# A graph layer on one core: three panels share the first groups of rows, and the late pieces of normalisation follow a new plan

## The chip, the cores and the metric

The kernel runs on one core of one Trainium2 chip. The metric is the device time of one execution in microseconds, as the median of several runs; lower is better.

## The reference

x is 8192 x 128, adj is 8192 x 8192 of zeros and ones (about one in 1024 is a one).

```
h    = relu(layernorm(x))                       # over the 128 features
deg  = max(adj.sum(axis=1), 1);  dis = deg ** -0.5
diff = (dis[:,None] * adj * dis[None,:]) @ h - h
sim  = h @ h.T / (|h_i| |h_j|)                  # cosines of all pairs of rows
attn = softmax(beta * sim * adj, axis=1)
out  = x + diff + sigmoid(alpha) * (attn @ h - h)
```

## The kernel before

The 8192 output rows are cut into 8 panels of 1024 (PANELS), the 8192 source rows into 4 groups (ch) of 16 tiles of 128. A **unit** is one panel with one tile of sources: a block of 128 x 1024 pairs. There are 512 units, numbered n = 0 to 511. ORDER lists (panel, group) for each chunk of 16 units, RUNS lists the stretches of chunks that keep one panel's accumulator in PSUM (panel, first chunk, end). Panels 0 and 1 share the first source group, so that the work can start before the other groups are normalised; where a panel's accumulator has been left, ScalarE has copied it to SBUF (`copy_acc`), and VectorE adds the later part (`add_acc`).

Each unit goes through the engines like this, always one instruction per step, with two or four buffers:

- TensorE, `cosines(n)` (L822): six 512-column matmuls of the unit vectors u, kept as fp16 head and tail (uT_hi, uT_lo), into one of two halves of cos_ps.
- VectorE, `masked(n)` (L693): the cosines times the adjacency bytes, to xm.
- ScalarE: two exponentials of it, the fp16 head (L418) and fp32 (L422).
- GpSimd, `rest(n)` (L325): the tail of the exponential by subtraction.
- TensorE, `sums(n)` (L867, L869, L871), called three units later (LAG): 24 matmuls that add e times h into the panel's accumulator.

Between these, VectorE transposes each block of adjacency words (`turn`, L630, every fourth unit) and sums the adjacency rows for the degrees (`sum_rows`, L637: 8 pieces a chunk, 256 in all; `sum_bytes` after every four chunks). GpSimd issues the row loads (L304, 8 a chunk, from `first_unit(k)` on) and makes the tails of h (L316, at the units of `tails`). SP stores the transposed adjacency and, by `keep_h`, h.

The first two groups of h are made ahead of the loop. The **late pieces** are the same steps for the others, put between units: `stats_of_x` (L508) and `mean_var` (L513) of x, a rough root on ScalarE (`var_root`) refined by `late_scale`, relu on ScalarE (L367, one tile a unit), `head_of_h` on ScalarE (L377), `stats_of_h` (L531) and `mean_var_of_h` (L536), `late_square_sums`, `ssq_root`, `late_norms`, `late_unit_rows` (L599), and at the units of AHEAD the transposition on TensorE (L798) of 1024 unit rows into the free half of cos_ps, copied from there by VectorE as head and tail (`copy_uT`, L606 and L607). The small steps pass through late_ps, a piece of PSUM. The order is written out by hand, by unit number: each engine runs its own loop over n. Ahead of the loop, TensorE runs WARM matmuls on the identity (L878, two passes each).

When all units are done, the roots of the degrees are made and a second phase (L901), 512 matmuls a panel, gives the diffusion. It is not touched by the change.

## Time and profile before

| | |
|---|---|
| median of 3 runs | 1890.43 us (1889.03 to 1893.34) |
| the profiled execution | 1890.3 us, span 1888.2 us |
| mean granted TensorE clock | 0.997 |
| busy: TensorE, VectorE, ScalarE, GpSimd | 97%, 66%, 68%, 67% |
| first cosine, last masked product | 38.88 us, 1426.26 us |
| second phase starts | 1436.65 us |

The span runs from the first to the last instruction. Matmuls overlap in their pipeline, so the busy time of one line of TensorE is more than its share, and the distance of starts is the better measure. The clock is given as a part of full speed (2.4 GHz).

### The profile page before, as it was taken

What the parts mean: (1) busy time and instruction counts of PE and PEld (TensorE: products, weight loads), DVE (VectorE), ACT (ScalarE), POOL (GpSimd) and SP (SyncE); (2) the same over time, 40 slices, a digit from 0 to 9 for tenths busy, and PEclk for the clock granted to TensorE, in tenths of its full rate; (3) what the DMA queues carried; (4) which work ended last, traced back from release to release, by engine and by line L of the source; (5) the groups of instructions that cost most, each with busy time, mean ns of one, the idle gap of its engine ahead of it and who ended that gap; (6) DMA issues with size and microseconds to landing.
All of it is one profiled execution on the core that took longest, in us unless ns stands there. A gap on an engine that the chain in (4) does not pass through costs nothing.

```text
span 1888.2 us, 44938 instructions
## 1 busy us (share of the span) xinstructions
PE 1835.1 (97%) x19614; PEld 1453.3 (77%) x19614; DVE 1253.8 (66%) x1591; ACT 1274.9 (68%) x1202; POOL 1272.0 (67%) x793
## 2 busy tenths in 40 slices
PE   4899999999999999999999999999998999999999
PEld 3667667777777777777777777777777888888888
DVE  7988997888787778778777877787876210111111
ACT  4879988888889889988998898898886000000000
POOL 4878899999999999999999999999882000000000
PEclk9999999999999999999999999999999999999999
DMA  9976877778896778888876778888436744555520
GB/s 153 171 90 91 135 91 96 96 95 105 102 127 91 102 93 100 107 101 104 105 101 90 102 95 100 107 101 108 99 108 251 242 171 162 198 177 175 205 101 12
DMA packets 190409, 229.39 MB, mean 121 GB/s; under 512 B 7940, under 2 KB 163588, under 8 KB 186116
## 3 DMA queue, kind: packets, MB, share of 16 engines
q0 software_dynamic: 135168, 67.13, 45.6%
q1 hardware_dynamic: 29380, 145.77, 21.3%
q10 hardware_dynamic: 25664, 13.63, 2.6%
q8 instruction: 153, 2.51, 0.5%
q14 instruction: 44, 0.36, 0.1%
HBM read 352.32 MB, written 75.50 MB: 227 GB/s over the span
## 4 chain that ended last, share of the span: by engine, by line
PE 87%; DVE 4%; ACT 3%; POOL 3%; issue 2%; DMA 0%; SPq 0%; DVEq 0%; POOLq 0%
PE cos_ps L822 31%; PE cos_ps L901 12%; PE top_ps L901 12%; PE top_ps L867 11%; PE top_ps L871 11%; PE top_ps L869 10%; POOL ustage L325 2%; ACT xe L422 1%; ACT ustage L418 1%; DVE xe L693 1%; DVE top_ps L637 1%; ACT asb L367 1%; PE cos_ps L878 1%; DVE ptmp L508 0%; POOL arena L304 0%
## 5 line engine op out<-in xcount | busy, mean ns | idle before, releaser
L325 POOL TENSOR_TENSOR ustage<-xe,ustage 128x1024 f16<-128x1024 f32 x512 | 1097.2, 2146 | 145.1 <-ACT xe L422 138.4
L693 DVE TENSOR_TENSOR xe<-cos_ps,arena 128x1024 f32<-128x1024 f32 x512 | 626.5, 1224 | 248.2 <-PE cos_ps L822 159.7
L418 ACT ACTIVATE ustage<-xe,ebias,ab 128x1024 f16<-128x1024 f32 x512 | 635.5, 1241 | 150.5 <-DVE xe L693 149.0
L867 PE MATMUL top_ps<-h,ustage 128*128 128x129 f16 x4096 | 720.6, 220 | 10.7 <-POOL ustage L325 7.3
L871 PE MATMUL top_ps<-h,ustage 128*128 128x129 f16 x4096 | 720.0, 220 | 0.0
L869 PE MATMUL top_ps<-hlo,ustage 128*128 128x128 f16 x4096 | 719.6, 219 | 0.0
L422 ACT ACTIVATE xe<-xe,ebias,ab 128x1024 f32<-128x1024 f32 x512 | 628.7, 1228 | 1.3 <-POOL ustage L325 1.2
L867 PEld LDWEIGHTS top_ps<-h,ustage 128*128 128x128 f16 x4096 | 401.4, 98 | 73.2 <-POOL ustage L325 17.0
L869 PEld LDWEIGHTS top_ps<-hlo,ustage 128*128 128x128 f16 x4096 | 401.3, 98 | 56.6 <-issue 0.6
L871 PEld LDWEIGHTS top_ps<-h,ustage 128*128 128x128 f16 x4096 | 401.3, 98 | 0.0
L822 PE MATMUL cos_ps<-uT_hi 128*128 128x512 f16 x1024 | 306.2, 381 | 13.1 <-DVE uT_lo L607 7.4
L637 DVE TENSOR_REDUCE top_ps<-arena 128x8 f32<-128x1024 uint16 x256 | 311.7, 1217 | 0.0
L822 PE MATMUL cos_ps<-uT_hi,uT_lo 128*128 128x512 f16 x1024 | 306.0, 380 | 0.0
L822 PE MATMUL cos_ps<-uT_lo,uT_hi 128*128 128x512 f16 x1024 | 305.9, 380 | 0.0
L822 PEld LDWEIGHTS cos_ps<-uT_hi,uT_lo 128*128 128x128 f16 x1024 | 116.5, 114 | 105.7 <-issue 1.6
L822 PEld LDWEIGHTS cos_ps<-uT_lo,uT_hi 128*128 128x128 f16 x1024 | 116.2, 113 | 106.0 <-issue 1.6
L304 POOL DMA_DIRECT2D arena<-adj_in_dram x256 | 171.6, 671 | 7.5 <-DMA asb<-x_in 7.5
L630 DVE STREAM_TRANSPOSE arena<-arena 128x1024 uint32<-128x1024 uint32 x128 | 158.0, 1234 | 0.0
L773 DVE SCALAR_TENSOR_TENSOR ptmp<-top_ps,dis,ptmp 128x128 f32<-128x128 f32 x64 | 19.5, 347 | 189.4 <-PE top_ps L901 188.8
L773 DVE SCALAR_TENSOR_TENSOR ptmp<-cos_ps,dis,ptmp 128x128 f32<-128x128 f32 x64 | 19.5, 347 | 157.8 <-PE cos_ps L901 157.2
L901 PE MATMUL cos_ps<-uT_hi,arena 128*128 128x256 f16 x896 | 98.5, 273 | 2.8 <-DVE uT_hi L754 2.8
L822 PEld LDWEIGHTS cos_ps<-uT_hi 128*128 128x128 f16 x1024 | 87.1, 113 | 16.7 <-DVE uT_lo L607 8.1
(113 smaller groups left out, 1043.7 us busy)
## 6 DMA issues: line engine op xcount, KB each, us to landing
arena<-adj_in_dram POOLq DMA_DIRECT2D x256, 256.0 KB, 8.1
at_scratch<-arena SPq DMA_DIRECT2D x128, 512.0 KB, 4.5
arena<-at_scratch SPq DMA_DIRECT2D x26, 2048.0 KB, 8.8
xe<-at_scratch SPq DMA_DIRECT2D x6, 2048.0 KB, 8.7
h_scratch<-asb SPq DMA_DIRECT2D x16, 256.0 KB, 8.7
arena<-h_scratch SPq DMA_DIRECT2D x16, 256.0 KB, 6.4
ustage<-h_scratch ACTq DMA_DIRECT2D x8, 512.0 KB, 4.1
ptmp<-x_in ACTq DMA_DIRECT2D x8, 512.0 KB, 5.3
```

The source lines that it names most:

```text
L304: pool.dma_start(rows8[k % RS][C * q:C * (q + 1), of, :], adj_v[panel][:, of, 2048 * ch + 512 * q:2048 * ch + 512 * (q + 1)]).then_inc(row ...
L325: nc.gpsimd.tensor_tensor(elo[:, n % ES, :], ef[:, n % XS, :], ehi[:, n % ES, :], ALU.subtract).then_inc(elo_done, 1)
L418: nc.scalar.activation(ehi[:, n % ES, :], xm[:, n % XS, :], ACT.Exp, bias=ebias[:, 0:1], scale=ab[:, 1:2]).then_inc(ehi_done, 1)
L422: nc.scalar.activation(ef[:, n % XS, :], xm[:, n % XS, :], ACT.Exp, bias=ebias[:, 0:1], scale=ab[:, 1:2]).then_inc(ef_done, 1)
L630: nc.vector.transpose(at_words[:, w, :].rearrange("p (a r) -> p a r", r=32), rows_words[k % RS][:, :, 32 * w:32 * (w + 1)]).then_inc(at_re ...
L637: nc.vector.tensor_reduce(out=pairs_ps[:, of], in_=rows_pairs[k % RS][:, 8 * part:8 * (part + 1), :], axis=AX.X, op=ALU.add).then_inc(rows ...
L693: nc.vector.tensor_tensor(xm[:, n % XS, :], cos_ps[:, slot_of(n), :], at8[:, m % W, :, n % B], ALU.mult).then_inc(x_done, 1)
L822: last = nc.tensor.matmul(cos_ps[:, slot_of(n), q * HALF:(q + 1) * HALF].rearrange("p (w z) -> p w z", w=W), own(mine, s), columns(src, pa ...
L867: nc.tensor.matmul(top_ps[:, bank, col:col + P + 1], head, h1[:, s, 0:P + 1], start=(first and t % 3 == 0), stop=final, skip_group_check=True)
L869: nc.tensor.matmul(top_ps[:, bank, col:col + P], head, hlo[:, s, :], start=False, stop=final, skip_group_check=True)
L871: last = nc.tensor.matmul(top_ps[:, bank, col:col + P + 1], tail, h1[:, s, 0:P + 1], start=False, stop=final, skip_group_check=True)
L901: return nc.tensor.matmul(acc2[panel % 2][:, t, :], slot8[k % SL][:, j // B, t * P:(t + 1) * P, j % B], y[s // 32][:, s % 32, :], start=(s ...
```

## The change

- **Order.** Panel 2 joins panels 0 and 1 in the first two source groups. The third group is first used at unit 96 (before 64), the fourth at 112 (before 80). There are three runs that VectorE adds (ADDED) and three early ones that ScalarE copies. AHEAD moves from units 18, 22, 56, 60, 73, 77 to 22, 30, 66, 78, 98, 106.
- **Plan.** The row sums start at unit 8 (SUM_UNITS) and take a third place in four between units 142 and 181. Row loads, `tails`, `keep_h` and every late piece get units of their own from tables. The variance of the third and fourth group is made in two halves (`late_var`, `late_scale`, `late_shift`), and copied to PSUM first. Relu runs in two units of three.
- **Head copies.** For the six late transpositions ScalarE copies the head (`copy_head`), ahead of its exponentials of that unit; VectorE waits for it and makes the tail.
- **Square sums.** `square_sums` works on the means and second moments that bn_stats gives for the halves of a tile; the sixteen bn_aggr fall away, early and late. The statistics of h go to PSUM (hstats is a view of late_ps, which is bank 3 of top_ps).
- **Warm-up.** WARM 24 in place of 40.

The diff, with unchanged lines and the declarations of buffers and semaphores left out; the rest of what is left out are the columns in which `sum_bytes` puts the first three batches, and `panel < 3` in `cosines`:

```diff
--- before.py
+++ after.py
@@ -38,7 +38,7 @@
-    WARM = 40
+    WARM = 24
@@ -47,12 +47,17 @@
-    AHEAD = {18: 2, 22: 3, 56: 4, 60: 5, 73: 6, 77: 7}
-    ORDER = [(0, 0), (1, 0), (1, 1), (0, 1), (0, 2), (0, 3), (1, 2), (1, 3)] + [(p, ch) for p in range(2, PANELS) for ch in range(CH)]
-    RUNS = [(0, 0, 1), (1, 1, 3), (0, 3, 6), (1, 6, 8)] + [(p, CH * p, CH * (p + 1)) for p in range(2, PANELS)]
+    AHEAD = {22: 2, 30: 3, 66: 4, 78: 5, 98: 6, 106: 7}
+    ORDER = [(0, 0), (1, 0), (1, 1), (2, 1), (2, 0), (0, 1), (0, 2), (0, 3), (1, 2), (1, 3), (2, 2), (2, 3)]
+    ORDER += [(p, ch) for p in range(3, PANELS) for ch in range(CH)]
+    RUNS = [(0, 0, 1), (1, 1, 3), (2, 3, 5), (0, 5, 8), (1, 8, 10), (2, 10, 12)] + [(p, CH * p, CH * (p + 1)) for p in range(3, PANELS)]
+    ADDED = (3, 4, 5)
...
+    SUM_UNITS = [n for n in range(8, UNITS) if n % B in (0, 3) and n != 72 or n % B == 2 and 142 <= n < 182][:8 * CHUNKS]
@@ -256,8 +262,8 @@
-                if m in (13, 16):
-                    keep_h(2 if m == 13 else 3)
+                if m in (14, 21):
+                    keep_h(2 if m == 14 else 3)
@@ -326,10 +332,10 @@
-                return 16 * (k - RS) + (18 if k < 13 else 13)
-            tails = {7: 4, 9: 5, 11: 6, 13: 7, 48: 8, 50: 9, 52: 10, 54: 11, 64: 12, 66: 13, 68: 14, 70: 15}
+                return max(16 * (k - RS) + 13, SUM_UNITS[8 * (k - RS) + 7] + 1)
+            tails = {7: 4, 9: 5, 11: 6, 13: 7, 44: 8, 47: 9, 54: 10, 57: 11, 70: 12, 73: 13, 80: 14, 83: 15}
@@ -356,13 +362,13 @@
-            def var_root(g, groups=1):
-                of = slice(16 * g, 16 * (g + groups))
+            def var_root(g):
+                of = slice(16 * g, 16 * (g + 1))
...
-                act.wait_ge(ln_ready, min(g, 2) + 1)
+                act.wait_ge(ln_ready, g + 1)
@@ -394,9 +400,9 @@
-                if run in (0, 4):
-                    groups = 1 if run == 0 else CH
+                if run in (0, 2, 6):
+                    groups = {0: 1, 2: 2, 6: CH}[run]
@@ -407,11 +413,17 @@
+            def copy_head(hb, slot):
+                act.wait_ge(uT_done, hb + 1)
+                nc.scalar.activation(uT_hi[:, PW * hb:PW * (hb + 1)], cos_ps[:, slot, :], ACT.Copy).then_inc(uT_hi_copied, 1)
...
-                if n >= 16 and n - LAG + 1 == 16 * RUNS[run][2] and run not in (2, 3):
+                if n >= 16 and n - LAG + 1 == 16 * RUNS[run][2] and run not in ADDED:
...
+                if n in AHEAD:
+                    copy_head(AHEAD[n], (slot_of(n) + 1) % 2)
@@ -422,16 +434,17 @@
-                if n in (3, 5, 45, 47, 61, 63):
-                    head_of_h({3: 2, 5: 3, 45: 4, 47: 5, 61: 6, 63: 7}[n])
-                elif n in (11, 49, 66):
-                    ssq_root({11: 1, 49: 2, 66: 3}[n])
-                elif n == 24:
-                    var_root(2, 2)
-                if 29 <= n < 45:
-                    relu(2, n - 29, n - 28)
-                elif 45 <= n < 61:
-                    relu(3, n - 45, n - 44)
+                if n in (3, 5, 38, 51, 64, 76):
+                    head_of_h({3: 2, 5: 3, 38: 4, 51: 5, 64: 6, 76: 7}[n])
+                elif n in (7, 55, 87):
+                    ssq_root({7: 1, 55: 2, 87: 3}[n])
+                elif n in (17, 39):
+                    var_root({17: 2, 39: 3}[n])
+                if 25 <= n < 49 and n % 3 != 0:
+                    relu(2, (n - 25) // 3 * 2 + (n - 25) % 3, (n - 25) // 3 * 2 + (n - 25) % 3 + 1)
+                elif 52 <= n < 76 and n % 3 != 0:
+                    relu(3, (n - 52) // 3 * 2 + (n - 52) % 3, (n - 52) // 3 * 2 + (n - 52) % 3 + 1)
@@ -531,18 +544,17 @@
-            def mean_var_of_h(g):
-                for s in range(16):
-                    ins = nc.vector.bn_aggr(out=hv[:, 16 * g + s, :], in_=hstats[:, s, :])
-                return ins
-            def early_square_sums(g):
+            def square_sums(g):
...
-                link(mean_var_of_h(g))
-                link(nc.vector.tensor_tensor(ssq[:, of], hv[:, of, 0], hv[:, of, 0], ALU.mult))
-                link(nc.vector.tensor_tensor(ssq[:, of], ssq[:, of], hv[:, of, 1], ALU.add))
-                nc.vector.tensor_scalar(ssq[:, of], ssq[:, of], float(P), COS_EPS * COS_EPS, ALU.mult, ALU.max).then_inc(hvar_ready, 1)
+                halves = hstats.rearrange("p s (k m) -> p s k m", m=3)
+                link(nc.vector.tensor_copy(hmeans, halves[:, :, :, 1]))
+                link(nc.vector.tensor_tensor(hmeans, halves[:, :, :, 1], hmeans, ALU.mult))
+                link(nc.vector.scalar_tensor_tensor(out=hmeans, in0=hmeans, scalar=P / 2.0, in1=halves[:, :, :, 2],
+                                                    op0=ALU.mult, op1=ALU.add))
+                link(nc.vector.tensor_reduce(out=late_ps[:, 0:16], in_=hmeans, axis=AX.X, op=ALU.add))
+                nc.vector.tensor_scalar(ssq[:, of], late_ps[:, 0:16], COS_EPS * COS_EPS, None, ALU.max).then_inc(hvar_ready, 1)
+                dve.wait_ge(hvar_ready, g + 1)
@@ -559,26 +571,25 @@
-            def late_scale(step):
-                of = slice(32, TILES)
+            def late_var(g):
+                of = slice(16 * g, 16 * (g + 1))
+                link(mean_var(g))
+                link(nc.vector.tensor_copy(late_ps[:, 0:16], mv[:, of, 1]))
+                nc.vector.tensor_scalar(va[:, of], late_ps[:, 0:16], LN_EPS, None, ALU.add).then_inc(var_ready, 1)
+                dve.wait_ge(var_ready, g + 1)
+            def late_scale(g, step):
+                of = slice(16 * g, 16 * (g + 1))
...
-                    dve.wait_ge(std_ready, 3)
-                if step < 3:
-                    late_step(va[:, of], vb[:, of], vc[:, of], rstd[:, of], step)
-                else:
-                    link(nc.vector.tensor_copy(late_ps[:, 0:32], rstd[:, of]))
-                    nc.vector.scalar_tensor_tensor(out=shift[:, of], in0=mv[:, of, 0], scalar=-1.0, in1=late_ps[:, 0:32],
-                                                   op0=ALU.mult, op1=ALU.mult).then_inc(ln_ready, 1)
-                    dve.wait_ge(ln_ready, 3)
-            def late_square_sums(g):
+                    dve.wait_ge(std_ready, g + 1)
+                late_step(va[:, of], vb[:, of], vc[:, of], rstd[:, of], step)
+            def late_shift(g):
...
-                both = late_ps[:, 32:64].rearrange("p (s k) -> p s k", k=2)
-                link(nc.vector.tensor_copy(both, hv[:, of, :]))
-                link(nc.vector.tensor_tensor(vc[:, of], hv[:, of, 0], both[:, :, 0], ALU.mult))
-                link(nc.vector.tensor_tensor(both[:, :, 0], vc[:, of], both[:, :, 1], ALU.add))
-                nc.vector.tensor_scalar(ssq[:, of], both[:, :, 0], float(P), COS_EPS * COS_EPS, ALU.mult, ALU.max).then_inc(hvar_ready, 1)
-                dve.wait_ge(hvar_ready, g + 1)
+                link(nc.vector.tensor_copy(late_ps[:, 0:16], rstd[:, of]))
+                nc.vector.scalar_tensor_tensor(out=shift[:, of], in0=mv[:, of, 0], scalar=-1.0, in1=late_ps[:, 0:16],
+                                               op0=ALU.mult, op1=ALU.mult).then_inc(ln_ready, 1)
+                dve.wait_ge(ln_ready, g + 1)
@@ -595,15 +606,18 @@
-                link(nc.vector.tensor_copy(late_ps[:, 64:72], rnorm[:, of]))
-                nc.vector.tensor_tensor(unit[hb], x_st[:, of, :], late_ps[:, 64:72].unsqueeze(2).to_broadcast([P, 8, P]),
+                link(nc.vector.tensor_copy(late_ps[:, 16:24], rnorm[:, of]))
+                nc.vector.tensor_tensor(unit[hb], x_st[:, of, :], late_ps[:, 16:24].unsqueeze(2).to_broadcast([P, 8, P]),
...
-                link(nc.vector.tensor_copy(uT_hi[:, of], cos_ps[:, slot, :]))
+                if hb < READY:
+                    link(nc.vector.tensor_copy(uT_hi[:, of], cos_ps[:, slot, :]))
+                else:
+                    dve.wait_ge(uT_hi_copied, hb - READY + 1)
@@ -613,7 +627,7 @@
-            early_square_sums(0)
+            square_sums(0)
@@ -694,50 +710,49 @@
-            piece = 0
+            XSTATS = {6: (2, 0, 4), 7: (2, 4, 9), 8: (2, 9, 10), 9: (2, 10, 11), 11: (2, 11, 12), 12: (2, 12, 13), 13: (2, 13, 14),
+                      14: (2, 14, 16), 24: (3, 0, 1), 25: (3, 1, 2), 27: (3, 2, 3), 28: (3, 3, 4), 29: (3, 4, 5), 31: (3, 5, 6),
+                      32: (3, 6, 7), 33: (3, 7, 8), 34: (3, 8, 13), 35: (3, 13, 14), 36: (3, 14, 15), 37: (3, 15, 16)}
+            HSTATS = {0: (1, 0, 4), 2: (1, 4, 8), 3: (1, 8, 12), 4: (1, 12, 16),
+                      46: (2, 0, 5), 47: (2, 5, 6), 48: (2, 6, 7), 49: (2, 7, 8), 50: (2, 8, 13), 51: (2, 13, 14), 52: (2, 14, 15), 53: (2, 15, 16),
+                      75: (3, 0, 1), 76: (3, 1, 2), 77: (3, 2, 3), 79: (3, 3, 4), 80: (3, 4, 5), 81: (3, 5, 6), 82: (3, 6, 11),
+                      83: (3, 11, 12), 84: (3, 12, 13), 85: (3, 13, 15), 86: (3, 15, 16)}
...
-                if n in (16 * RUNS[2][2] + LAG - 1, 16 * RUNS[3][2] + LAG - 1):
-                    add_acc(2 if n < 16 * RUNS[3][2] else 3)
+                for run in ADDED:
+                    if n == 16 * RUNS[run][2] + LAG - 1:
+                        add_acc(run)
...
-                elif (n % B in (0, 3) or n in (134, 138, 142, 146, 150)) and piece < 8 * CHUNKS:
+                elif n in SUM_UNITS:
+                    piece = SUM_UNITS.index(n)
...
-                    piece += 1
-                if 1 <= n < 9:
-                    stats_of_h(1, 2 * n - 2, 2 * n)
-                elif 31 <= n < 47:
-                    stats_of_h(2, n - 31, n - 30)
-                elif 48 <= n < 64:
-                    stats_of_h(3, n - 48, n - 47)
-                if 6 <= n < 22:
-                    g, o = 2 + (n - 6) // 8, (n - 6) % 8
-                    stats_of_x(g, 2 * o, 2 * (o + 1))
-                    if o == 7:
-                        link(mean_var(g))
-                if n in (9, 47, 64):
-                    link(mean_var_of_h({9: 1, 47: 2, 64: 3}[n]))
-                elif n in (10, 48, 65):
-                    late_square_sums({10: 1, 48: 2, 65: 3}[n])
-                elif n in (12, 13, 14):
-                    late_norms(1, n - 12)
-                elif n in (50, 51, 52):
-                    late_norms(2, n - 50)
-                elif n in (67, 68, 69):
-                    late_norms(3, n - 67)
-                elif n == 23:
-                    nc.vector.tensor_scalar(va[:, 32:TILES], mv[:, 32:TILES, 1], LN_EPS, None, ALU.add).then_inc(var_ready, 1)
-                elif n in (25, 26, 27, 28):
-                    late_scale(n - 25)
-                elif n in (15, 19, 53, 57, 70, 74):
-                    late_unit_rows({15: 2, 19: 3, 53: 4, 57: 5, 70: 6, 74: 7}[n])
-                elif n == 100:
+                if n in XSTATS:
+                    stats_of_x(*XSTATS[n])
+                if n in HSTATS:
+                    stats_of_h(*HSTATS[n])
+                if n in (15, 38):
+                    late_var(2 if n == 15 else 3)
+                elif n in (19, 20, 21, 41, 42, 43):
+                    late_scale(2 if n < 30 else 3, (n - 19) % 22)
+                elif n in (23, 45):
+                    late_shift(2 if n == 23 else 3)
+                elif n in (6, 54, 86):
+                    square_sums({6: 1, 54: 2, 86: 3}[n])
+                elif n in (10, 58, 90):
+                    for step in range(2):
+                        late_norms({10: 1, 58: 2, 90: 3}[n], step)
+                elif n in (14, 61, 93):
+                    late_norms({14: 1, 61: 2, 93: 3}[n], 2)
+                elif n in (18, 26, 62, 70, 94, 102):
+                    late_unit_rows({18: 2, 26: 3, 62: 4, 70: 5, 94: 6, 102: 7}[n])
+                elif n == 130:
...
-                if n in (TILES - 1, 2 * TILES - 1):
-                    sum_bytes(n // TILES)
+                if n in (74, 138):
+                    sum_bytes(n // TILES - 1)
@@ -815,7 +830,7 @@
-                if panel < 2 and n % 8 == 0:
+                if panel < 3 and n % 8 == 0:
@@ -846,19 +862,19 @@
-                if first and run in (1, 2):
+                if first and 0 < run <= ADDED[0]:
...
-                elif first and run in (3, 4):
-                    pe.wait_ge(acc_added, run - 2)
+                elif first and run and run - 1 in ADDED:
+                    pe.wait_ge(acc_added, run - len(ADDED))
...
-                    pe.wait_ge(acc_copied, run - 2)
+                    pe.wait_ge(acc_copied, run - len(ADDED))
...
-                if panel < 2 and n % 4 == 0:
+                if panel < 3 and n % 4 == 0:
...
```

## Rows read from the trace of the kernel before

**Rows 1.** The page, busy time, share of the span and instructions of each engine.

```profile
PE 1835.1 (97%) x19614; PEld 1453.3 (77%) x19614; DVE 1253.8 (66%) x1591; ACT 1274.9 (68%) x1202; POOL 1272.0 (67%) x793
```

**Rows 2.** Busy time by stretch: stretch, its us, each engine's, granted clock, DMA share, GB/s.

```profile
110.00:130.00 20.00, 17.60 (x182) 13.09 (x180) 17.56 (x36) 13.86 (x14) 15.53 (x13) 0.91 1.02 119
...
600.00:800.00 200.00, 200.00 (x2268) 152.29 (x2267) 158.08 (x137) 180.16 (x155) 184.20 (x112) 1.00 0.75 98
```

**Rows 3.** TensorE's waits: line, who released it, us in all, times, longest.

```profile
PE cos_ps L822 <- DVE uT_lo L607: 7.4, 4, 4.1
...
PE top_ps L867 <- POOL ustage L325: 7.3, 12, 1.3
```

**Rows 4.** Timeline of VectorE, masked products 0, 81 and 511: start, us, instruction.

```profile
41.65 1.23 DVE L693 TENSOR_TENSOR xe<-cos_ps,arena 128x1024 f32<-128x1024 f32 x1 [1.68 <-PE cos_ps L822]
...
284.16 1.23 DVE L693 TENSOR_TENSOR xe<-cos_ps,arena 128x1024 f32<-128x1024 f32 x1 [0.29 <-PE cos_ps L822]
...
1426.26 1.23 DVE L693 TENSOR_TENSOR xe<-cos_ps,arena 128x1024 f32<-128x1024 f32 x1 [1.43 <-PE cos_ps L822]
```

**Rows 5.** Timeline around unit 81 (TensorE, ScalarE, GpSimd), undisturbed.

```profile
282.61 0.59 PE L822 MATMUL cos_ps<-uT_hi 128*128 128x512 f16 x2
...
286.57 1.23 ACT L422 ACTIVATE xe<-xe,ebias,ab 128x1024 f32<-128x1024 f32 x1
...
287.87 2.14 POOL L325 TENSOR_TENSOR ustage<-xe,ustage 128x1024 f16<-128x1024 f32 x1 [0.51 <-ACT xe L422]
...
290.55 0.59 PE L822 MATMUL cos_ps<-uT_hi 128*128 128x512 f16 x2
```

**Rows 6.** Timeline of VectorE, units 40 to 42.

```profile
162.21 1.23 DVE L693 TENSOR_TENSOR xe<-cos_ps,arena 128x1024 f32<-128x1024 f32 x1 [0.45 <-DVE ptmp L531]
163.35 1.22 DVE L637 TENSOR_REDUCE top_ps<-arena 128x8 f32<-128x1024 uint16 x1
164.48 0.28 DVE L531 BATCH_NORM_STATS2 ptmp<-asb 128x6 f32<-128x128 f32 x1
...
165.94 1.23 DVE L630 STREAM_TRANSPOSE arena<-arena 128x1024 uint32<-128x1024 uint32 x1
167.10 0.25 DVE L531 BATCH_NORM_STATS2 ptmp<-asb 128x6 f32<-128x128 f32 x1
```

**Rows 7.** Timeline of the start, TensorE and VectorE.

```profile
22.49 10.54 PE L878 MATMUL cos_ps<-ident 128*128 128x128 f32 x80 [17.75 <-ACT asb L367]
...
24.10 1.17 DVE L536 BATCH_NORM_AGGREGATE hv<-ptmp 128x2 f32<-128x6 f32 x16
...
31.16 0.17 DVE L525 SCALAR_TENSOR_TENSOR shift<-mv,rstd 128x16 f32<-128x16 f32 x1
...
33.94 1.23 DVE L606 CAST uT_hi<-cos_ps 128x1024 f16<-128x1024 f32 x1 [2.60 <-PE cos_ps L798]
...
38.88 0.96 PE L822 MATMUL cos_ps<-uT_hi 128*128 128x512 f16 x2 [4.10 <-DVE uT_lo L607]
```

**Rows 8.** Timeline of TensorE, the late transposition of unit 73.

```profile
258.87 1.04 PE L798 MATMUL cos_ps<-ident,ptmp 128*128 128x128 f32 x8
259.74 0.59 PE L822 MATMUL cos_ps<-uT_hi 128*128 128x512 f16 x2
```

**Rows 9.** Groups of instructions from 38 to 290 us: count, busy us, mean ns, idle before.

```profile
L304 POOL DMA_DIRECT2D arena<-adj_in_dram x32 | 21.5, 673 | 0.0
...
L367 ACT ACTIVATE asb<-asb,shift,rstd 128x128 f32<-128x128 f32 x34 | 16.2, 479 | 0.0
...
L316 POOL TENSOR_TENSOR hlo<-asb,h 128x512 f16<-128x512 f32 x12 | 13.5, 1127 | 0.0
...
L377 ACT ACTIVATE h<-asb 128x1024 f16<-128x1024 f32 x6 | 6.2, 1040 | 0.0
```

**Rows 10.** A stretch as in group 2, and TensorE's cosines just before it.

```profile
94.00:98.00 4.00, 4.00 (x31) 2.58 (x30) 3.93 (x6) 1.96 (x2) 3.35 (x2) 0.62 0.35 134
...
93.61 1.04 PE L822 MATMUL cos_ps<-uT_hi 128*128 128x512 f16 x2 [1.69 <-DVE xe L693]
```

22 lines of the change are left out of this document (13 added, 9 removed).

## The prediction

> **What bounds the kernel now.** I read the page's busy shares first: TensorE is busy 97% of the span, the other engines about two thirds [rows 1]. Then the busy times by stretch of the span: from 400 us on TensorE has hardly an idle moment, while between 110 and 130 us it is busy for 17.6 of 20 us, at a mean granted clock of 0.91, and VectorE for 17.6 of 20 as well [rows 2]. So time can only be won in the first 290 us. TensorE's waits name VectorE (the head and tail copies of u, 7.4 us) and GpSimd (the tails of the exponentials, 7.3 us) [rows 3]. The last view counts: the masked product (L693) runs once a unit, so its starts are a clock of the unit loop. Undisturbed, one unit takes (290.55 - 282.61) / 3 = 2.647 us, which is 6 cosine and 24 sum matmuls [rows 5]. From unit 0 at 41.65 to unit 81 at 284.16 the trace has 242.5 us where 81 x 2.648 = 214.5 would do: 28.0 us lost. By unit 511, at 1426.26, it is 1384.6 against 1353.1, a loss of 31.5 [rows 4]. Those 31.5 us are the most that anything inside the loop can give.
>
> Some of them stay. The six late transpositions take TensorE 0.87 us each [rows 8], 5.2 in sum; the two degree products take about 0.8 of the last ten units (my estimate from the unit distances there); about 2.7 us are lost after unit 81, at ends of runs and at the second byte sum.
>
> **Why VectorE is late, and what the change makes of it.** Start to start, a masked product takes VectorE 1.14 us, a row sum 1.13, a turn 1.16, one bn_stats 0.3 [rows 6]. A head or tail copy of 1024 columns takes about 1.2, sixteen bn_aggr 1.2, a small operation 0.17, about 0.21 with its own wait [rows 7]. Add up units 16 to 23 of before: 8 masked 9.1, 4 sums 4.5, 2 turns 2.3, 6 pairs of bn_stats 3.1, sixteen aggregates 1.2, two pairs of copies 4.8, one set of unit rows 1.5, the variance step 1.2: 27.7 us, where TensorE's eight units take 21.2. So VectorE is 6.5 us over. In the same way units 8 to 15 are 6.1 over, 48 to 63 7.0, 64 to 79 1.4; 24 to 47 are 6.9 under, but what TensorE has idled is not won back.
>
> In the new plan units 16 to 23 have masked 9.1, sums 4.5, turns 2.3, twelve small operations 2.5, unit rows 1.5, one tail copy 1.1: 21.1 us, 0.1 under. Every other block of eight from 0 to 207 comes out under as well, except 8 to 15, 0.5 over. Four things make that: the row sums start at unit 8 and are made up at units 142 to 182, where blocks have 5.2 us free; the sharing by three panels moves the need for the third group's transposed rows from unit 64 to 96, so the late pieces spread over 107 units and not 78; the head copies, 6 x 1.2, go to ScalarE; the square sums drop sixteen aggregates for one small operation more (5 x 0.2 in place of 1.2 + 4 x 0.2, 1 us each). The variance in two halves costs twelve small operations more, 2.5 us, and these lie within the blocks' slack. bn_stats now writes PSUM: no row shows that; between 0.28 us as in SBUF and, by the row sum that writes PSUM after reading eight times as much, 1.2 us. I take 0.28, as the written part is 6 elements in both; at twice that, units 46 to 53 would use up their 1.5 us of slack and cost about 1 us more.
>
> **Start, -3.3 us.** 80 warm-up passes take 10.54 us from 22.49 [rows 7]; WARM 24 makes 48, 6.3 us, until 28.8. The early square sums save 1.2 - 0.4 = 0.75 us of the chain ahead, so both sets of unit rows are there by about 29.9, and the second transposition ends at 30.8. VectorE's own chain ends with the second shift, at 31.33 before and 30.6 now. Before, the first head copy waited for TensorE until 33.94; now it starts at 30.6. The four copies stay behind each other on VectorE, so the first cosine moves from 38.88 to about 35.5. Before, the adjacency rows were there by then (the first turn did not wait); I expect the same at 35.5.
> First units, gain against the distances of before: unit 8 came at 41.65 + 20.6, as VectorE was full with sums and statistics. With TensorE and ScalarE as bounds (eight cosines 10.3 us, five sums 6.8, and 1.9 us in which the first sum's tail is made) it is at +19.2, so the new count starts at -2.0 where before had -0.6.
>
> **New stalls, the largest cost: +11.1 us.** At a unit n of AHEAD the order is: TensorE transposes into the free half of cos_ps (0.87), runs cosines(n) and sums(n-3), and cosines(n+1) waits for uT_copied. The head copy stands in ScalarE's queue behind both exponentials of unit n-1. Count from the start of cosines(n-1): masked product at +1.55 (284.16 against 282.61), first exponential at +2.8, second at +3.96, its successor at +5.1 [rows 4, 5]. The head copy takes 1.04 as the row of a ScalarE copy of 1024 columns [rows 9] (from SBUF; the exponentials' 1.23 is the upper end), so VectorE begins the tail at +6.2, and cosines(n+1) can start at +7.5. TensorE would be there at 2.65 + 0.87 + 2.65 = +6.17. Stall: 1.33 us, six times 8.0. With both copies on an idle VectorE it would be nil (start at 3.77, two copies of 1.25, +6.3). What is late on top: VectorE is 1.2 us behind at unit 22 (units 15 to 21 carry 3.9, 2.3, 2.3, 2.6, 3.1, 2.9, 2.9); the relu between exponentials and copy at 30 and 66, 0.39 each; the head of h at 64 leaves ScalarE 1.0 behind at 66, and 0.2 at 78. Sum 3.1. Behind the waiting tail copy stands masked(n), 5.8 us after its predecessor, and behind that the exponentials; their sums come three units later, so nothing more is lost.
>
> **GpSimd, +2.4.** A tail subtraction takes 2.10 us start to start, a row issue 0.68, a tail of h 1.1 [rows 5, 9]. Tail subtraction 81 ends at 290.0, and sums(81) start behind cosines(84), at 290.55 + 1.29 = 291.84: 1.8 us of slack [rows 5]. Units 40 to 47 now carry eight row issues and the tails at 44 and 47: 8 x 2.78 + 2.2 = 24.5 - 21.2 = 3.3 us, plus ScalarE's 0.8 of lag after the head of h at 38, less 1.83: about 2.2 of stall; 56 to 63 add 0.2. Before had tails and issues together too (48 to 55 and 64 to 71, each 4.1 over), and the row of 7.3 us is that.
>
> **Late and rest, +3.8.** The 2.7 us after unit 81 stay; one accumulator copy and one addition more than before, 0.6 (a copy of three banks fits in the 1.3 us behind a sum, almost); 0.5 for masked products that VectorE's small overloads (15, 41, 74) delay. The extra 32-column degree product is nothing that a row would show. keep_h moves on SP's queue past one store of transposed rows for the third group and past five for the fourth, to units 53 and 81, its eight issues still behind each other (7 us); the next reader is a copy after unit 258, so this costs nothing.
>
> **Sum.** Loss within the loop: -2.0 + 5.2 + 0.8 + 11.1 + 2.4 + 3.8 = 21.3, against 31.5: 10.2 won. With 3.3 at the start 13.5. The profiled execution took 1890.3 us (span 1888.2), 0.1 from the runs' median, so the forecast is 1876.8.
>
> **Rivals.**
> Head copies for free (0.22): if the waits of the six units lie in slack that I don't see (ScalarE ahead of my count), 11.1 us less: 1865.7. For it speaks that ScalarE is busy only two thirds; against it that its queue is in order and both exponentials are bound to the product before.
> The clock falls after each new stall (0.12): at 93.61 us, after 1.69 us without work, a pair of cosine matmuls took 1.04 us, with a mean of 0.62 granted between 94 and 98 us, so about the lower level of 1.2 GHz [rows 10]. At the full clock the pair takes 0.59 [rows 5]. Three pairs lose 1.35 us, six times that 8.1: 1884.9. Against it: a stall of 1.3 us stands alone between full units, and the one in the trace followed others.
> The Trainium skill ("TensorE: Matmul & The Clock Gate", Part 1) says that the low clock is the default and that activity releases it, which speaks against a shorter warm-up and against added idle time; the trace agrees in that the fall at 94 us follows idle time.
> VectorE was not what held the first units (0.10): if the chain through ScalarE and GpSimd holds the pace once VectorE is lighter (ScalarE's blocks of eight are within 0.7 us of TensorE's 21.2 from unit 24 to 55), only the start is won: 1887.
> Slower (0.04): ScalarE's second exponential of n-1 also waits for GpSimd's tail of n-3; from a GpSimd lag of 1.9 us at an AHEAD unit on, that wait passes straight into the head copy. If the lag were 4.8 at all six, each stall would be 4.2 us and the sum 17 us worse: 1894. I find a lag of 2 at most, at 78.
> The forecast itself 0.52, own range 1872 to 1882 (a head copy of 1.23, GpSimd's stall nil or double).
>
> **Range and chances.** From the free copies at 1865.7, with 2 below for GpSimd's stall, to the case of falling clocks at 1884.9 and 1 above: 1864 to 1886; outside stay the last two rivals. 0.2% is 3.8 us, about what a measurement of this kernel can tell. Faster takes the forecast, the first rival and most of the second: 0.84; within 0.2% 0.12; slower 0.04.
>
> **What the new profile would show.** Unit 0's masked product at about 38.4; L878 with 48 passes ending at 28.8; masked products 2.65 apart from unit 8 on, with gaps of 5.8 us only at 22, 30, 66, 78, 98 and 106; TensorE's waits led by the tail copy, 8 to 11 us beside the start; the wait for GpSimd at 2 to 3 us. Wrong it would be if gaps of 4 us stood elsewhere (a statistic in PSUM that costs more), if the cosines after an AHEAD unit ran at half clock, or if the wait for the tail copy were missing.

## The result and the profile after

The changed kernel took 1884.34 us in the median of 6 runs (1882.24 to 1885.31). The kernel before, timed beside it on the same chips, has a median of 1892.76 us over six runs, and the ratio is 0.9961, 95% interval 0.9951 to 0.9971: 0.4% faster, 7.4 us, from 5.5 to 9.3. The profiled execution took 1885.31 us (span 1883.2 against 1888.2, mean clock 0.995 against 0.997), and it is the slowest of the six; its span fell by 5.0 us, where 13.5 were forecast for it.

The page after, busy shares, answers to [rows 1], and two of its stretches to [rows 2]:

```profile
PE 1833.1 (97%) x19584; PEld 1453.0 (77%) x19584; DVE 1247.8 (66%) x1546; ACT 1279.8 (68%) x1209; POOL 1271.7 (68%) x793
```

```profile
110.00:130.00 20.00, 18.34 (x212) 14.29 (x210) 16.36 (x19) 17.22 (x18) 17.16 (x13) 1.00 1.10 128
224.00:228.00 4.00, 2.07 (x6) 0.77 (x7) 2.36 (x2) 1.51 (x2) 2.01 (x1) 0.76 1.06 162
600.00:800.00 200.00, 200.00 (x2262) 152.04 (x2260) 158.35 (x137) 179.88 (x155) 184.80 (x115) 1.00 0.76 99
1420.00:1440.00 20.00, 15.27 (x164) 13.11 (x162) 17.82 (x30) 15.84 (x48) 4.52 (x3) 0.91 0.67 242
```

From 110 to 130 us VectorE is now busy for 16.36 us and not 17.56, and the clock stays at 1.00. Two other stretches carry a clock under 1: 224 to 228 us, where TensorE was busy for 2.07 of 4 us, and the one in which the second phase begins.

TensorE's waits (line, released by, us in all, times, longest) answer to [rows 3]:

```profile
PE cos_ps L837 <- DVE uT_lo L621: 14.0, 7, 4.1
...
PE top_ps L883 <- POOL ustage L331: 3.7, 5, 1.3
```

The wait for the tail copy has doubled, from 7.4 to 14.0 us, and GpSimd's has halved. Masked products 0, 81 and 511, as in [rows 4]:

```profile
39.40 1.22 DVE L709 TENSOR_TENSOR xe<-cos_ps,arena 128x1024 f32<-128x1024 f32 x1 [1.76 <-PE cos_ps L837]
...
271.07 1.22 DVE L709 TENSOR_TENSOR xe<-cos_ps,arena 128x1024 f32<-128x1024 f32 x1
...
1419.58 1.23 DVE L709 TENSOR_TENSOR xe<-cos_ps,arena 128x1024 f32<-128x1024 f32 x1 [1.42 <-PE cos_ps L837]
```

From unit 0 to 511 it is 1380.2 us, 27.1 over 511 x 2.648, where before had 31.5 and the forecast 21.3. The first product comes at 39.40, 2.25 us earlier than before (forecast 3.3), and behind the last one 1.7 us are lost that before did not lose: 2.25 + 4.4 - 1.7 = 5.0.

The rest of this document reads from the same count, made for every kernel from the starts of the masked products in its trace. Each entry is (start of unit n) - (start of unit 0) - 2.648 n in us, the time lost up to unit n. The AHEAD units are 22, 30, 66, 78, 98 and 106 in all but the first kernel, so a loss between 64 and 72, say, is that of unit 66. From 80 to 96 no kernel loses anything.

| kernel | start of unit 0 | 8 | 16 | 24 | 32 | 48 | 56 | 64 | 72 | 80 | 104 | 112 | 136 | 511 |
|---|---|---|---|---|---|---|---|---|---|---|---|---|---|---|
| before | 41.65 | -0.6 | 5.5 | 14.2 | 14.3 | 15.1 | 20.0 | 23.4 | 24.3 | 28.0 | 28.4 | 28.4 | 29.3 | 31.5 |
| changed | 39.40 | -1.2 | -0.3 | 1.8 | 4.6 | 4.6 | 6.8 | 6.9 | 12.4 | 17.2 | 19.4 | 21.6 | 24.1 | 27.1 |
| heads_between | 37.92 | -1.2 | -0.3 | 0.7 | 1.9 | 1.9 | 4.1 | 4.3 | 6.5 | 8.6 | 9.7 | 10.8 | 13.3 | 16.2 |
| heads_on_vector | 39.37 | -1.2 | -0.3 | 1.3 | 3.1 | 3.1 | 5.3 | 5.4 | 6.7 | 8.4 | 9.5 | 10.6 | 13.1 | 16.1 |
| place_at_100 | 37.68 | -1.2 | -0.3 | 1.9 | 4.6 | 4.6 | 6.8 | 7.0 | 12.4 | 15.6 | 20.6 | 22.4 | 22.8 | 25.8 |
| warm_fill | 37.91 | -1.2 | -0.3 | 1.8 | 4.6 | 4.6 | 6.8 | 6.9 | 12.3 | 15.5 | 17.8 | 20.0 | 22.5 | 25.4 |
| stall_fill | 39.69 | -1.2 | -0.3 | 1.9 | 4.6 | 4.6 | 6.8 | 6.9 | 10.6 | 13.9 | 16.1 | 18.4 | 20.9 | 23.8 |
| place_on_scalar | 38.14 | -1.2 | -0.3 | 0.7 | 1.9 | 1.9 | 4.1 | 4.3 | 6.5 | 8.6 | 9.7 | 10.8 | 11.2 | 14.1 |
| tails_apart | 39.66 | -1.2 | -0.3 | 0.7 | 2.0 | 2.3 | 2.7 | 2.7 | 4.8 | 6.9 | 8.0 | 9.1 | 11.5 | 14.5 |
| warm_40 | 41.75 | -1.2 | -0.4 | 0.7 | 1.9 | 1.9 | 4.1 | 4.2 | 6.5 | 8.5 | 9.6 | 10.7 | 13.3 | 16.2 |
| sums_from_0 | 37.78 | 1.4 | 1.9 | 3.0 | 4.2 | 4.5 | 4.2 | 5.4 | 7.4 | 10.3 | 11.4 | 12.5 | 15.0 | 17.9 |
| combined | 37.84 | -1.2 | -0.3 | 0.7 | 2.0 | 2.3 | 2.7 | 2.7 | 4.8 | 6.8 | 7.9 | 9.0 | 9.4 | 12.3 |
| combined_filled | 37.49 | -1.2 | -0.3 | 0.7 | 1.9 | 2.3 | 2.7 | 2.7 | 4.8 | 6.8 | 7.9 | 9.0 | 9.4 | 12.3 |

Unit 66 of the changed kernel, where most is lost (timeline: start, us, instruction, idle before it and who ended it):

```profile
218.42 1.24 ACT L434 ACTIVATE xe<-xe,ebias,ab 128x1024 f32<-128x1024 f32 x1
219.56 1.04 ACT L383 ACTIVATE h<-asb 128x1024 f16<-128x1024 f32 x1
220.51 0.48 ACT L373 ACTIVATE asb<-asb,shift,rstd 128x128 f32<-128x128 f32 x1
220.90 1.23 ACT L430 ACTIVATE ustage<-xe,ebias,ab 128x1024 f16<-128x1024 f32 x1
222.03 1.23 ACT L434 ACTIVATE xe<-xe,ebias,ab 128x1024 f32<-128x1024 f32 x1
223.16 0.48 ACT L373 ACTIVATE asb<-asb,shift,rstd 128x128 f32<-128x128 f32 x1
223.55 1.00 ACT L418 ACTIVATE uT_hi<-cos_ps 128x1024 f16<-128x1024 f32 x1
...
224.65 1.23 DVE L621 TENSOR_TENSOR uT_lo<-cos_ps,uT_hi 128x1024 f16<-128x1024 f32 x1 [3.71 <-ACT uT_hi L418]
225.79 1.22 DVE L709 TENSOR_TENSOR xe<-cos_ps,arena 128x1024 f32<-128x1024 f32 x1
...
221.55 0.59 PE L837 MATMUL cos_ps<-uT_hi,uT_lo 128*128 128x512 f16 x2
...
225.93 0.98 PE L837 MATMUL cos_ps<-uT_hi 128*128 128x512 f16 x2 [2.44 <-DVE uT_lo L621]
226.71 1.06 PE L837 MATMUL cos_ps<-uT_lo,uT_hi 128*128 128x512 f16 x2
```

ScalarE makes a head of h and a relu behind unit 64, then both exponentials of unit 65, a relu, and only then, at 223.55, the head copy. The tail follows at 224.65, and TensorE, idle since 223.49, starts at 225.93 after 2.44 us of idle time. Its pairs of cosines then take 0.98 and 1.06 us, not 0.59: the clock has fallen to the lower level, 1.2 GHz (0.76 granted in the mean from 224 to 228 us).

The six pauses behind the transpositions lasted 1.51, 1.66, 2.44, 1.99, 1.14 and 1.14 us. Cosines at half rate followed those of 66 and 78 alone.

### The profile page after: what moved, and what is told of

It reads as the page before. It is cut to its first block, busy times and chain, and to the rows that moved or that the text cites. A ratio compares the mean times of both kernels' runs of the same rounds, so it can differ in the third digit from the quotient of the medians.

```text
span 1883.2 us, 44861 instructions
## 1 busy us (share of the span) xinstructions
PE 1833.1 (97%) x19584; PEld 1453.0 (77%) x19584; DVE 1247.8 (66%) x1546; ACT 1279.8 (68%) x1209; POOL 1271.7 (68%) x793
## 3 DMA queue, kind: packets, MB, share of 16 engines
q1 hardware_dynamic: 29380, 145.77, 21.3%
## 4 chain that ended last, share of the span: by engine, by line
PE 87%; POOL 5%; DVE 3%; issue 2%; ACT 2%; DMA 0%; SPq 0%; DVEq 0%; POOLq 0%; ACTq 0%
PE cos_ps L837 31%; PE cos_ps L917 12%; PE top_ps L917 12%; PE top_ps L883 11%; PE top_ps L887 11%; PE top_ps L885 11%; POOL ustage L331 5%; DVE xe L709 1%; POOL arena L310 1%; ACT xe L434 1%; DVE uT_lo L621 0%; PE cos_ps L894 0%; DMA asb<-x_in 0%; ACT asb L373 0%; ACT uT_hi L418 0%
## 5 line engine op out<-in xcount | busy, mean ns | idle before, releaser
L788 DVE SCALAR_TENSOR_TENSOR ptmp<-top_ps,dis,ptmp 128x128 f32<-128x128 f32 x64 | 19.5, 347 | 189.4 <-PE top_ps L917 188.8
L788 DVE SCALAR_TENSOR_TENSOR ptmp<-cos_ps,dis,ptmp 128x128 f32<-128x128 f32 x64 | 19.5, 346 | 158.5 <-PE cos_ps L917 157.9
L837 PEld LDWEIGHTS cos_ps<-uT_hi 128*128 128x128 f16 x1024 | 87.4, 113 | 18.4 <-DVE uT_lo L621 15.2
```

The costliest lines, as they stand in the source:

```text
L837: last = nc.tensor.matmul(cos_ps[:, slot_of(n), q * HALF:(q + 1) * HALF].rearrange("p (w z) -> p w z", w=W), own(mine, s), columns(src, pa ...
```

## The experiments

Each is compared with the kernel before the change, timed again beside it on the same chip; every experiment has four runs. The median of the kernel before moved by 2 us between these occasions, so between kernels of different occasions the ratios compare better than the medians. The changed kernel has 1884.34 against 1892.76, 0.9961.

| kernel | median us | before us | ratio | 95% interval |
|---|---|---|---|---|
| heads_between | 1872.32 | 1892.34 | 0.9896 | 0.9879 to 0.9912 |
| heads_on_vector | 1872.81 | 1892.34 | 0.9896 | 0.9882 to 0.9911 |
| place_at_100 | 1883.04 | 1892.34 | 0.9951 | 0.9936 to 0.9966 |
| warm_fill | 1882.31 | 1892.34 | 0.9946 | 0.9931 to 0.9961 |
| place_on_scalar | 1871.00 | 1890.99 | 0.9892 | 0.9877 to 0.9907 |
| tails_apart | 1872.85 | 1890.99 | 0.9898 | 0.9883 to 0.9913 |
| warm_40 | 1876.48 | 1890.99 | 0.9918 | 0.9903 to 0.9932 |
| sums_from_0 | 1874.30 | 1890.99 | 0.9907 | 0.9891 to 0.9924 |
| stall_fill | 1880.71 | 1890.66 | 0.9943 | 0.9927 to 0.9960 |
| combined | 1867.44 | 1890.66 | 0.9879 | 0.9865 to 0.9894 |
| combined_filled | 1867.07 | 1890.66 | 0.9875 | 0.9860 to 0.9890 |

### heads_between: the head copy between the two exponentials

```diff
-                if n in AHEAD:
-                    copy_head(AHEAD[n], (slot_of(n) + 1) % 2)
...
+                if n + 1 in AHEAD:
+                    copy_head(AHEAD[n + 1], (slot_of(n + 1) + 1) % 2)
```

> The changed kernel, with each late head copy on ScalarE moved from behind both exponentials of unit n-1 to between them. Theory A (the stall after an AHEAD unit comes from the head copy's place in ScalarE's queue): TensorE's waits for the tail copy, 14.0 us with 4.1 at the start, fall to about 5; the pause of 2.44 us at unit 67 goes and with it the half-clocked cosines behind it; the loop from the first to the last masked product falls from 1380.2 to about 1369, the time by 9 to 12 us, to about 1873. Theory B (the pieces around it, relu and heads of h on ScalarE, hold the unit anyway): the wait moves to GpSimd's tails, since each second exponential comes 1.0 us later, and the time falls by less than 3 us.

```profile
PE cos_ps L837 <- DVE uT_lo L621: 6.3, 4, 4.1
...
PE top_ps L883 <- POOL ustage L331: 3.6, 5, 1.3
```

Theory A. The same instructions in another place give 0.9896 where the change gave 0.9961. The waits for the tail copy fall from 14.0 to 6.3 us (5 were expected), of which 4.1 are those of the start; the pause of 2.44 us is one of 0.92, and the cosines behind it run at full rate; the wait for GpSimd, which theory B saw growing, is 3.6 after 3.7. The loss in the loop goes from 27.1 to 16.2 us. At the two AHEAD units that stand free, 98 and 106, an AHEAD unit costs 1.1 us and no longer 2.2, of which 0.87 is the transposition itself.

### heads_on_vector: the head copies back on VectorE

```diff
-                if n in AHEAD:
-                    copy_head(AHEAD[n], (slot_of(n) + 1) % 2)
...
-                if hb < READY:
-                    link(nc.vector.tensor_copy(uT_hi[:, of], cos_ps[:, slot, :]))
-                else:
-                    dve.wait_ge(uT_hi_copied, hb - READY + 1)
+                link(nc.vector.tensor_copy(uT_hi[:, of], cos_ps[:, slot, :]))
```

> The changed kernel, with the late head copies back on VectorE, behind the transposition, as before; the rest of the plan stays. Theory A (the hand-over to ScalarE costs 1.3 us and more at each of six units): the plan leaves VectorE 0.4 us at these units, the copy needs 1.2, so VectorE falls behind by 0.9 and no wait of TensorE over 0.5 us is left; the time falls by 7 to 11 us. Theory B (the head copy had to leave VectorE, since it is full): masked products fall behind over the following eight units, 1.2 us at each of the six; the time stays or rises by up to 4 us.

```profile
PE cos_ps L832 <- DVE uT_lo L616: 6.3, 4, 4.1
```

Theory A again. This kernel is the change without its third part, and it is 1.0% faster than before. So the plan, the sharing by three panels, the square sums and the warm-up are together worth about 19.5 us, and handing the head copies to ScalarE the way the change did it took 12 of these back, with what the clock lost behind the two longest pauses among them. Of the four only the warm-up is measured by itself (warm_40, below); what the plan, the sharing by three panels and the square sums are worth singly, no experiment says. VectorE had room for the head copies: the loss grows by at most 1.1 us against heads_between (at units 32 to 56), and falls under it by unit 80. Pauses of 0.97, 0.67 and 0.55 us are left, where none over 0.5 was expected.

### place_at_100 and place_on_scalar: who copies the placing matrix

In place_at_100 the unit rows of unit 102 lie in the same memory as the placing matrix and overwrite it, so the degrees are placed with other numbers; the instructions are the same. place_on_scalar stands on heads_between.

```diff
-                elif n == 130:
+                elif n == 100:
```

> The changed kernel, with the four copies of the placing matrix made at unit 100 as before, not at 130 behind the accumulator's addition. They took 1.4 us in all in the trace of before and 4.4 in that of the changed kernel. Theory A (two pieces of VectorE work in one unit exceed the slack): masked product 131 comes 2.7 us after 130 plus at most 1, not 6.9, and the loss of 2.5 us between units 128 and 136 falls to under 1.3; the time falls by 1 to 2 us. Theory B (the loss comes from the addition and the row sums after it): the gap at 130 shrinks but the count at unit 136 stays.

```diff
+                if n == 110:
+                    act.wait_ge(uT_done, HB)
+                    spread = ident32[:, :].rearrange("k (c b) -> k b c", b=B)
+                    for q in range(Q):
+                        nc.scalar.activation(place[:, :, q, :], spread, ACT.Copy).then_inc(place_ready, 1)
...
-                elif n == 130:
-                    make_place()
```

> As heads_between, with the four copies of the placing matrix made by ScalarE at unit 110, and not by VectorE at 130. On VectorE one of the four took 3.8 us of the 4.4, beside two tail subtractions of GpSimd back to back; made at unit 100 they took 4.1 us. Theory A (VectorE's copy from SBUF to SBUF waits while GpSimd works, wherever it stands): on ScalarE the four take about 1.1 us in all, the loss of 2.5 us between units 128 and 136 falls to about 0.4, and the time falls by 2 us, to about 1870.3. Theory B (the loss is that of the accumulator's addition at 130): the loss stays at 2 us or more.

The changed kernel at unit 130, VectorE, and GpSimd beside it:

```profile
406.61 1.36 DVE L686 TENSOR_TENSOR asb<-top_ps,asb 128x387 f32<-128x387 f32 x3
407.88 4.38 DVE L676 COPY ptmp<-ident 128x128 f32<-128x128 f32 x4
412.19 1.21 DVE L709 TENSOR_TENSOR xe<-cos_ps,arena 128x1024 f32<-128x1024 f32 x1
...
407.35 4.23 POOL L331 TENSOR_TENSOR ustage<-xe,ustage 128x1024 f16<-128x1024 f32 x2
```

In place_at_100 theory A was right on unit 130 and wrong on the gain. The loss between units 128 and 136 falls from 2.5 to 0.4 us, but between 96 and 104 it grows from 2.2 to 5.0: the four copies take 4.1 us there, beside another pair of GpSimd's subtractions. They were cheap in the kernel before, where GpSimd issued a row behind its subtraction at that moment. So what costs is not that two pieces meet in one unit: each of the long copies ends within 0.15 us of the end of one of GpSimd's subtractions. The 1.3 us by which the loop is still shorter (25.8 against 27.1) are not a gain of the move: between units 72 and 80, ahead of the edit, this execution kept its clock behind unit 78 and lost 1.6 us less. On ScalarE the copies take 0.42 to 0.43 us each, the loss between 128 and 136 is 0.4 us too, nothing comes back elsewhere, and the whole count falls by 2.1 us, to 14.1, where 2 were foretold. In the medians (1871.00 after 1872.32) this is within their spread; the count shows it.

### tails_apart: GpSimd's queue

On heads_between.

```diff
-            tails = {7: 4, 9: 5, 11: 6, 13: 7, 44: 8, 47: 9, 54: 10, 57: 11, 70: 12, 73: 13, 80: 14, 83: 15}
+            tails = {7: 4, 9: 5, 11: 6, 13: 7, 39: 8, 49: 9, 52: 10, 54: 11, 70: 12, 73: 13, 80: 14, 83: 15}
```

> As heads_between, with the tails of h of GpSimd moved from units 44, 47, 54, 57 to 39, 49, 52, 54, so that none stands beside the row issues of units 40 to 47. Theory A (GpSimd's queue makes the loss of 2.2 us between units 48 and 56): 40 to 47 are then 1.1 us over the pace and within the slack of 1.8, the loss falls to 0.5 or less, TensorE's waits for GpSimd from 3.6 to about 1.5 us, the time by 1.7 to 2.2 us. Theory B (ScalarE's accumulator copy at 50 and head of h at 51 make it): the loss stays.

```profile
PE top_ps L883 <- POOL ustage L331: 3.0, 4, 1.3
```

Theory A: from unit 48 to 56 it loses 0.4 us and no longer 2.2, and 1.7 us of that last to the end (14.5 against 16.2). The waits put down to GpSimd fall only from 3.6 to 3.0 us, not to 1.5; the rest is a pause of 1.08 us at 176.87 us in heads_between, for which the profile names no releaser, and which is gone here. The median did not move, 1872.85 after 1872.32, and the profiled execution is 1.6 us longer: its unit 0 came 1.7 us later (39.66), with the first twelve cosine matmuls at half clock, and its second phase lost another 1.6 us to the clock. A gain of 1.7 us and the clock's own spread are of one size here, so the gain is shown by the count and not by the time.

### warm_40 and warm_fill: the start

warm_40 stands on heads_between, warm_fill on the changed kernel.

```diff
-    WARM = 24
+    WARM = 40
```

> As heads_between, with 40 warm-up matmuls as before the change. Theory A (the warm-up's length sets when the first transposition begins): it ends at about 32.3 to 33, unit 0's masked product comes at about 39.8 to 40.5, not 37.9, and the time rises by 2 to 2.5 us. Theory B (the low clock of the first microseconds and the chain of VectorE set it): masked product 0 moves by less than 1 us. The clock at the start differed by itself between runs by up to 1.5 us, so the start of the transposition is what decides.

```diff
+            for k in range(16):
+                nc.tensor.matmul(top_ps[:, 0, 0:P], ident32[:, :], ident32[:, :], start=True, stop=True)
```

> The changed kernel, with 16 added matmuls on the identity (32 passes, about 3.5 us) between the second transposition and the first cosines, into a bank that the first sum overwrites. In the trace of the changed kernel TensorE idled for 4.1 us there, and the next twelve cosine matmuls ran at half clock, to 41.65 us. Theory A (the idle time lets the clock fall): the first cosines run at 0.22 us each, masked product 0 comes at about 38.1 and not 39.4, sums(0) 1.3 us earlier, and the time falls by about 1.3 to 2 us. Theory B (the clock falls or comes back whatever runs before): masked product 0 stays at 39.4 or later, and the time is unchanged within 0.5 us.

The start of the changed kernel (answers to [rows 7]) and of heads_between, which differ in nothing there:

```profile
22.37 8.32 PE L894 MATMUL cos_ps<-ident 128*128 128x128 f32 x48 [17.89 <-ACT asb L373]
30.53 1.91 PE L813 MATMUL cos_ps<-ident,xe 128*128 128x128 f32 x16
36.54 1.04 PE L837 MATMUL cos_ps<-uT_hi 128*128 128x512 f16 x2 [4.10 <-DVE uT_lo L621]
...
41.65 0.65 PE L837 MATMUL cos_ps<-uT_hi 128*128 128x512 f16 x2
...
31.61 1.23 DVE L618 CAST uT_hi<-cos_ps 128x1024 f16<-128x1024 f32 x1 [1.00 <-PE cos_ps L813]
```

```profile
22.53 7.57 PE L894 MATMUL cos_ps<-ident 128*128 128x128 f32 x48 [18.07 <-ACT asb L373]
29.94 1.91 PE L813 MATMUL cos_ps<-ident,xe 128*128 128x128 f32 x16
35.95 0.62 PE L837 MATMUL cos_ps<-uT_hi 128*128 128x512 f16 x2 [4.10 <-DVE uT_lo L621]
...
36.84 0.98 PE L837 MATMUL cos_ps<-uT_hi,uT_lo 128*128 128x512 f16 x2
...
40.17 0.67 PE L837 MATMUL cos_ps<-uT_hi 128*128 128x512 f16 x2
```

With 40 matmuls the warm-up takes 10.55 us, the transposition begins at 32.98 and unit 0 comes at 41.75, which is theory A. The 3.8 us (and 4.2 in the median, 1876.48 after 1872.32) are more than the 2 to 2.5 that I gave: 3.0 of them are the later start of the transposition (32.98 after 29.94), and 0.8 are cosines that ran longer at half clock. The 48 passes took 8.32 us in one trace and 7.57 in the other. Passes of one form last 0.42 us at first (the very first 0.55) and 0.27 later, and start 0.21 and then 0.11 us apart: up to 28 us the changed kernel has 11 of them in 2 us (the windows of 24 to 28 us) and then 20, heads_between has 11, then 17, then 20, and warm_40 has 20 from 26 us on. So the first passes run at half rate, though the granted clock stands at 1.00 in all these windows, and the moment of the change differs from one execution to another: it lies between 25.4 and 28.5 us in the thirteen traces. In the pause before the first cosines the granted clock falls, in the first trace ahead of them (0.73 from 34 to 36 us, 0.50 from 36 on), in the second while they run (0.73 from 36 to 38 us), after five of them.

warm_fill fills that pause:

```profile
32.06 3.74 PE L898 MATMUL top_ps<-ident 128*128 128x128 f32 x32
36.32 0.62 PE L837 MATMUL cos_ps<-uT_hi 128*128 128x512 f16 x2 [0.52 <-DVE uT_lo L621]
36.78 0.59 PE L837 MATMUL cos_ps<-uT_lo,uT_hi 128*128 128x512 f16 x2
37.21 0.59 PE L837 MATMUL cos_ps<-uT_hi,uT_lo 128*128 128x512 f16 x2
```

All the cosines run at full rate, 0.59 to 0.62 us a pair, so it is the pause without work that lets the clock fall. Unit 0 comes at 37.91 and not 39.40, but the next seven units do not come earlier for it than in heads_between (unit 8 at 57.88 in both), since the first sum waits for the chain through ScalarE and GpSimd. So the fill is worth what the clock would have cost in that execution, 0 to 1.5 us; the time fell by 2 us against the changed kernel (1882.31), at the limit of what these runs tell. The profiled execution gained 3.2 us, but 1.6 of them lie at unit 78, where it kept its clock and which the edit does not touch.

### sums_from_0: the count by blocks

On heads_between.

```diff
-    SUM_UNITS = [n for n in range(8, UNITS) if n % B in (0, 3) and n != 72 or n % B == 2 and 142 <= n < 182][:8 * CHUNKS]
+    SUM_UNITS = [n for n in range(UNITS) if n % B in (0, 3) and not 64 <= n <= 72 or n % B == 2 and 142 <= n < 182][:8 * CHUNKS]
```

> As heads_between, with the row sums from unit 0 on, as before the change, and five places of the plan after unit 63 left empty in their stead. Theory A (the count of VectorE's work by blocks): units 0 to 7 carry 4.5 us more, 22.6 in all against TensorE's 21.2, but they were 3.1 under; unit 16's masked product comes 1 to 2 us later, and all of it stays in the time: 1 to 2 us slower. Theory B (the first units wait for ScalarE and GpSimd, so the sums fit between): unit 16 comes within 0.3 us of where it did, and the time does not change.

Theory A early: up to unit 16 only the row sums differ, unit 8 comes 2.6 us later against its unit 0 (1.4 and not -1.2), unit 16 2.2, and until unit 48 it stays at 2.2 to 2.6. The price at the end is not clean. `first_unit` takes the units of GpSimd's row issues from SUM_UNITS, so the edit also moved these issues eight units ahead (to 16, 32, 48 and 64 and the seven units behind each). At 48 to 56, where heads_between loses 2.2 us to issues and tails in 40 to 47, this kernel loses nothing, and at unit 56 the two are level (4.2 and 4.1). It then loses 1.1 us more between 56 and 64 and 0.8 between 72 and 80, with TensorE waiting for GpSimd for 4.9 us in all and not 3.6. So the 1.7 us that it is behind at unit 511, and the 2.0 in the median (1874.30 after 1872.32), are what is left of two moves. That four row sums of 1.13 us in a full block cost 2.2 us at once is shown; what they cost in the end, with the issues left where they were, is not.

### stall_fill: the clock after the pauses

```diff
+                if n in (66, 78):
+                    for k in range(10):
+                        nc.tensor.matmul(top_ps[:, 2, 384:512], ident32[:, :], ident32[:, :], start=False, stop=True, skip_group_check=True)
```

> The changed kernel, with 10 matmuls on the identity (20 passes, 2.2 us) on TensorE behind sums(n-3) at n = 66 and 78, into columns that nothing reads, so in the time in which cosines(n+1) wait for the tail copy. In the changed kernel these two pauses were followed by cosines at half clock. Theory A (a stall of over 2 us makes the clock fall, and that costs 1.3 to 1.6 us each): unit 72 minus unit 64 takes 1.3 us less than the 5.43 over the pace, unit 80 minus 72 about 3.2 over it and not 4.8, the time falls by 1.3 to 3 us. Theory B (the fall is not tied to the pause): half-clocked cosines appear there or elsewhere all the same, and the time stays within 1 us.

```profile
224.00:228.00 4.00, 3.85 (x34) 3.03 (x34) 2.62 (x3) 1.51 (x2) 2.23 (x2) 1.00 1.09 181
264.00:268.00 4.00, 4.00 (x41) 2.85 (x40) 3.80 (x5) 4.00 (x5) 3.43 (x3) 1.00 1.17 100
...
223.56 2.45 PE L907 MATMUL top_ps<-ident 128*128 128x128 f32 x20
226.16 0.62 PE L837 MATMUL cos_ps<-uT_hi 128*128 128x512 f16 x2 [0.15 <-DVE uT_lo L621]
226.62 0.59 PE L837 MATMUL cos_ps<-uT_lo,uT_hi 128*128 128x512 f16 x2
```

Theory A. The wait for the tail copy is as long as it was, but TensorE works through it, the clock stays at 1.00, and units 64 to 72 lose 3.8 us and no longer 5.4, units 72 to 80 3.3 and no longer 4.8; the count ends 3.25 us lower. The median is 1880.71, 3.6 under the changed kernel's. place_at_100 and warm_fill agree without a filler: their clock fell behind unit 66 and not behind 78, and they lose 5.4 and 3.2 us at the two places.

### combined and combined_filled

combined is heads_between with the edits of place_on_scalar and tails_apart. combined_filled adds the matmuls of warm_fill and these:

```diff
                 if k == 0:
                     pe.wait_ge(x_done, UNITS)
+                    for f in range(12):
+                        nc.tensor.matmul(cos_ps[:, 0, 0:P], ident32[:, :], ident32[:, :], start=True, stop=True)
```

> heads_between, place_on_scalar and tails_apart in one kernel. Theory A (their gains lie at different units and add up): loop from masked product 0 to 511 at 12.4 us over the pace (16.2 less 2.1 less 1.7), time 1869, which is 1.1 to 1.2% under the kernel before the change. Theory B (one frees what the next then takes): the count is above 14.

> combined, with matmuls on the identity in two of TensorE's pauses: 16 between the second transposition and the first cosines, 12 (24 passes, 2.6 us) between the last sum and the second phase. Theory A (the pauses make the clock fall in some executions, at the start for 3 to 5 us of cosines, at the second phase for 1.7 us in all): the two places run at full clock in every execution, the mean time falls by 1 to 2.5 us against combined and its spread narrows. Theory B (most of the low clock is hidden by the first sum's wait): less than 0.7 us.

```profile
PE cos_ps L840 <- DVE uT_lo L626: 6.3, 4, 4.1
...
PE top_ps L886 <- POOL ustage L331: 2.5, 3, 1.3
```

The gains add up: 12.3 us are lost in the loop where 12.4 were expected, and the time is 1867.44 us, 1.2% under the kernel before (ratio 0.9879) and 15.5 us (by the ratios) to 17 (by the medians) under the changed one. The added matmuls give 0.4 us more in the median, under what these runs can tell apart; their executions lie closer together (1866.84 to 1867.73 against 1867.29 to 1869.70), on four runs each. Theory B holds for the size. In the profile of combined the second phase kept its clock anyway; the first cosines ran at half rate from 36.9 to 40.1 us, and unit 0 came 0.35 us later than in combined_filled (37.84 and 37.49).

## Why the prediction was right or wrong

The direction was right, the size was not: 7.4 us by all runs (5.5 to 9.3) and 5.0 in the profiled spans, against 13.5. Two signs that the prediction had named for being wrong came: cosines at half clock behind an AHEAD unit, and a gap of over 4 us elsewhere (6.9 at unit 130). The steps that held:

- **VectorE's count by blocks.** Units 8 to 32 lost 14.9 us before and 5.8 after (3.2 in heads_between). Outside the AHEAD units the plan runs at TensorE's pace but for 0.9 us at units 8 to 16, 2.2 at 48 to 56 (GpSimd) and 2.5 at 128 to 136 (the copies). sums_from_0 shows the count from the other side as far as unit 48.
- **The stall of an AHEAD unit.** 1.33 us and 0.87 for the transposition make 2.2; the units that stand free, 98 and 106, cost 2.2 each, though the pauses themselves were 1.14 us. The head copy took 1.00 us, 1.04 was taken. That the sum of the pauses is near (9.9 us, 11.1 forecast) is in part luck: with what the prediction adds as late, unit 22 was given 2.5 us and had 1.51, unit 78 was given 1.5 and had 1.99.
- **GpSimd.** 2.2 us at units 40 to 47 and 0.2 at 56 to 63 were forecast; the count grows by 2.2 between 48 and 56 and by 0.2 between 56 and 64.

What failed, from the largest on:

- **The clock was taken at full speed in the sum.** The rival "the clock falls after each new stall" got 0.12, because a stall of 1.3 us would stand alone. The four pauses of 1.14 to 1.66 us did stay without a fall. But my own count gave 66 a pause of 2.7 us (1.33, 0.39 for the relu, 1.0 for the head of h; measured 2.44), and I did not ask the question again for that one. There the clock fell, and again behind the 1.99 us of unit 78. stall_fill puts the price of both at 3.25 us. The sum for the six units was 11.1 us and 14.4 came out (19.6 lost there, less 5.2 for the transpositions), of which 66 and 78 have 8.5. That is the step that failed most: the pauses were there as forecast, and the clock behind them, put at nothing in the sum, cost the 3.3.
- **Behind the loop** the forecast had nothing. After the 2.85 us before the second phase, its first panel took 57.6 us where it took 55.9 before: 1.7 us at the lower clock, after the same pause as before the change (2.83 us). That one goes with the execution: the pause stands in twelve of the thirteen traces, and the clock fell behind it in eight, not in the kernel before, heads_between, heads_on_vector and combined.
- **The start** came 1.05 us later than forecast: I gave the warm-up 0.132 us a pass, the mean over 80. The first passes take twice as long as the later ones, and the shorter warm-up had no fewer of the long ones (26 of its 48, against 13 of 80 before). The warm-up began at 22.37 and took 8.32 us, the transposition began at 30.5 and not at 28.8, and VectorE waited 1.00 us for it.
- **The copies at unit 130** have no term in the sum; they took 4.4 us and cost 2.1. Behind unit 112 the forecast allowed 4.1 us (0.8, 2.7 and 0.6) and 5.4 were lost: 1.3.
- **The first units** were at -1.2 and not -2.0, and units 8 to 16 lost 0.9 where 0.5 was given for such overloads: 1.2. The clock is not the reason for the first: warm_fill, with every cosine at full rate, has the same -1.2.

Together 3.3 + 1.7 + 1.05 + 1.3 + 1.2 = 8.5 us, the distance between 13.5 and 5.0. About 5 of these are the clock's (3.3 + 1.7). It differs between executions of one kernel (0.995 to 0.997 in the mean over six runs, and the fastest is 3 us under the profiled one), so the forecast's distance to the median is smaller than to the profile.

The rival "head copies for free" was wrong for this kernel: ScalarE had the time, but not at the place in its queue where the copy stood. Moved by one instruction, the copies were almost free, and the result came to 1872.3. The rival that VectorE was not what held the first units (0.10) fails on units 8 to 32, which lose 9.1 us less with a lighter VectorE. The rival on the clock had its mechanism right and its extent wrong: two of the six units, at 1.6 us each, and not all six at 1.35.

## What to carry to other kernels

When work moves to an engine with time to spare, count not its load but what stands before it in its queue at the moment when it is needed; here the same copy cost 1.1 us more a unit behind the second exponential than ahead of it (2.2 and 1.1 at units 98 and 106), and more where the clock fell. Count the load of the fullest helper engine by blocks of the bound engine's time: what a block over the pace loses, a block under it does not give back (before, 14.2 us at unit 24 and 15.1 at unit 48, in blocks that were 6.9 us under by my count). And size every pause of TensorE by itself, not by the mean: here the two longest of the six, 2.44 and 1.99 us, cost another 3.25 us in the clock, while the shorter ones cost no more than themselves. Length alone does not settle it, as the last section shows, so such a price is a chance and not a sum.

## What the runs showed of the hardware that was not expected

- One VectorE copy of 128 x 128 from SBUF to SBUF lasted 3.83 us, beside 0.26 for its neighbours, exactly while GpSimd ran two subtractions without a pause (407.35 to 411.6 us). In place_at_100 two such copies took 1.61 and 2.21 us, each up to the end of one subtraction. The row sums and masked products, with an operand or the result in PSUM, kept their 1.22 us beside subtractions of the same form. The Trainium skill ("GPSIMD Engine Reference", Key points) says that GpSimd shares its SBUF interfaces with VectorE, in contention with VectorE instructions in a two-port mode or with two SBUF inputs. The trace agrees in that the copy, from SBUF to SBUF, is what suffers; whether it ran in such a mode no row shows. It also shows that the copy waited through both subtractions, the second of which began 0.06 us before the first had ended.
- In the profiled execution of the changed kernel the clock fell behind the pauses of 2.44 and 1.99 us at units 66 and 78, and not behind those of 1.51, 1.66 and 1.14 at 22, 30, 98 and 106; in place_at_100 and warm_fill the same pause at 78 stayed without a fall. In the kernel before it fell behind pauses of 1.69 us (at 93.61) and 2.40 (at 113.49), the first of them soon after others, and stayed at 1.00 behind one of 2.48 us (at 193.27). So the length of a pause alone does not tell; the same instructions meet both outcomes in different executions, and a difference of 1 to 3 us between two kernels can be the clock's alone.
- TensorE's first passes took 0.42 us each, 0.21 from start to start, and the later ones 0.27, 0.11 from start to start, while the granted clock read 1.00 for both; the long ones went on from about 22.5 us to 25.4 in one execution and to 28.5 in another.
- bn_stats writing to PSUM took what it takes to SBUF (sixteen in 3.62 us, 3.59 before); the prediction had taken 0.28 us for one, and it was 0.28.
